# The last two tiles of a mixture-of-experts combine move to TensorE, their loads go in halves from two queues, and the written order of all steps is new

## The reference

```python
x = x + attention(layernorm(x), ...)                 # 16 heads, low-rank q and kv, rotary, causal softmax
x = x + smooth_quant_mlp(layernorm(x), fside, ctx)   # per batch: two int8 products, gate and up, then down
x = x + moe(layernorm(x), ...)                       # 32 experts, top 4 of 3 groups, and a shared MLP
```

```python
s = sqrt(max(amax_x, EPS) / max(amax_w, EPS))        # per column, over rows of x and of w
xs, ws = x / s, w * s
x_scale = max(max(abs(xs), axis=-1), EPS) / 127      # a maximum of each row of x
w_scale = max(max(abs(ws), axis=-1), EPS) / 127      # and of each row of the weights
out = round(xs / x_scale) @ round(ws / w_scale).T * x_scale * w_scale.T
```

## Time and profile before

| | us |
|---|---|
| median of 3 runs (lowest, highest) | 394.71 (391.9, 395.4) |
| the profiled execution, its own time | 394.67 |
| its span, first to last instruction | 392.8 |
| PE busy | 326.6 |
| DVE busy | 263.9 |
| ACT busy | 173.8 |
| POOL busy | 100.5 |

### The profile page before, as it was taken

How to read it: one execution, slowest core, us unless ns; L and a number is a source line. 1 busy time by engine, 2 the same in 40 slices (tenths; PEclk the granted TensorE clock), 3 DMA queues, 4 the chain that set the end, 5 groups by cost and what they waited for, 6 DMA issues and landing times.

```text
span 392.8 us, 6578 instructions
## 1 busy us (share of the span) xinstructions
PE 326.6 (83%) x2000; PEld 230.0 (59%) x2000; DVE 263.9 (67%) x1066; ACT 173.8 (44%) x538; POOL 100.5 (26%) x144
## 2 busy tenths in 40 slices
PE   1898999799999789898899899669684897989880
PEld 0555566566866556766566675447573775655660
DVE  2337686775578778788997778795686478334327
ACT  1233566677446755345786435772042230223100
POOL 4112212231030112025233005330016302545500
PEclk9899999999999989999999999999899798999995
DMA  7999592020000000000000000062000400090175
GB/s 261 332 408 361 166 393 112 0 81 2 2 2 0 2 2 2 0 1 26 14 9 5 2 1 2 15 236 81 0 2 3 138 13 0 7 331 18 32 238 195
DMA packets 17895, 34.28 MB, mean 87 GB/s; under 512 B 4780, under 2 KB 9513, under 8 KB 17220
## 3 DMA queue, kind: packets, MB, share of 16 engines
q1 hardware_dynamic: 15556, 32.66, 24.0%
q0 software_dynamic: 2304, 1.20, 1.1%
HBM read 27.10 MB, written 11.99 MB: 100 GB/s over the span
## 4 chain that ended last, share of the span: by engine, by line
PE 52%; DVE 16%; issue 15%; ACT 6%; POOL 5%; DMA 4%; SPq 1%; another core or an unknown queue 0%; POOLq 0%; DVEq 0%; ACTq 0%
PE psum L527 41%; PE psum L536 11%; DVE x_residual L1526 2%; POOL expert_rows L1612 2%; DMA region_a<-token_parts 2%; DVE region_t L1176 1%; DMA x_residual<-in_x_dram 1%; ACT region_t L933 1%; ACT region_r L881 1%; DVE region_t L1184 1%; DVE region_t L1174 1%; POOL rstd L1571 1%; DVE bn_stats L1074 1%; ACT region_t L931 1%; DVE region_t L1165 1%
## 5 line engine op out<-in xcount | busy, mean ns | idle before, releaser
L527 PE MATMUL psum<-region_h,region_b 128*128 128x256 f32 (+1 forms) x320 | 66.4, 343 | 3.4 <-ACT region_b L881 2.2
L527 PE MATMUL psum<-region_c,region_h 128*128 128x512 f32 x128 | 61.6, 606 | 0.5 <-issue 0.5
L931 ACT ACTIVATE region_t<-region_t,neg_max 128x128 f32<-128x128 f32 x64 | 25.6, 399 | 65.4 <-DVE neg_max L1176 65.0
L527 PEld LDWEIGHTS psum<-region_h,region_b 128*128 128x128 f32 x320 | 47.0, 191 | 11.2 <-issue 4.4
L1583 POOL TENSOR_TENSOR q_chunk<-q_chunk,q_rope_tmp 128x256 f32<-128x256 f32 x32 | 23.5, 734 | 110.3 <-DVE q_chunk L1155 110.2
L1612 POOL DMA_INDIRECT expert_rows<-h_moe,slot_scatter x32 | 32.5, 1016 | 25.4 <-issue 14.4
L536 PE MATMUL psum<-consts,region_t 128*128 128x128 f32 x192 | 32.2, 277 | 6.5 <-DVE region_t L1184 3.1
L527 PEld LDWEIGHTS psum<-region_c,region_h 128*128 128x128 f32 x128 | 23.2, 195 | 18.9 <-issue 18.0
L536 PEld LDWEIGHTS psum<-consts,region_t 128*128 128x128 f32 x192 | 23.0, 141 | 17.6 <-issue 12.4
L933 ACT ACTIVATE region_t<-region_t,neg_max 128x256 f32<-128x256 f32 x64 | 31.6, 494 | 0.0
L527 PE MATMUL psum<-w_folded_out,region_g 128*128 128x256 f32 x128 | 29.8, 381 | 0.0
(11 more groups left out here) (189 smaller groups left out, 616.0 us busy)
## 6 DMA issues: line engine op xcount, KB each, us to landing
region_a<-in_experts_dram SPq DMA_DIRECT2D x17, 384.0 KB, 5.9
region_b<-in_experts_dram SPq DMA_DIRECT2D x10, 384.0 KB, 6.1
region_a<-in_fold_dram SPq DMA_DIRECT2D x3, 1152.0 KB, 12.9
token_parts<-region_g SPq DMA_DIRECT2D x12, 256.0 KB, 6.0
region_a<-token_parts SPq DMA_DIRECT2D x6, 512.0 KB, 6.8
region_c<-in_experts_dram SPq DMA_DIRECT2D x5, 384.0 KB, 3.4
expert_rows<-region_g SPq DMA_DIRECT2D x10, 132.5 KB, 11.1
region_h<-expert_rows SPq DMA_DIRECT2D x5, 256.0 KB, 3.8
```

The source lines that it names most:

```text
L527: return nc.tensor.matmul(out_, lhsT, rhs, start=first, stop=last)
L931: nc.scalar.activation(pr[:, 0:P], pr[:, 0:P], ACT.Exp, bias=nmax[:, hn, 0:1], scale=-1.0, accum_out=sums[:, hn, 0:1])
```

## The change

1. The tiles 4 and 5 (`SUMMED`) are no longer added by `combine.4`. A step `weigh.0` has DVE make 8 diagonal matrices, the identity times the tokens' weights for one k, and `sum.t` is 4 products on PE, diagonal k by the rows of k, summed in PSUM, and one addition on DVE.
2. Each tile's load from `token_parts` is two DMAs, ranks k = 0, 1 and ranks k = 2, 3, with a semaphore each. Even tiles are loaded and stored by SP, odd ones by ACT. Who reads waits for each half.
3. `x_back` has 6 parts in place of 4: maximum, scaling and reciprocal of the rows, then the same for the weights, and `x_qscale` waits for each.
4. `ORDER` is new in the whole. Among it: `slot_weights` stands behind `send.3`, `gate_up.3` and `down.1`; `xpT.2` behind `s_down.2`; `send.3` behind `send.2`; `down.3` ahead of `gate_up.5`; `down.5` ahead of `hidT.6`; 13 one-hots behind `gate_up.7` in place of 12.

The diff in its core (the old and the new text of the order are cut to parts of their ends):

```diff
+SUMMED = (4, 5)
...
-r_pos.3 dispatch r_slots.3 r_slots.3+1 r_slots.3+2 r_slots.3+3 r_slots.3+4 scatter.3.0 send.0 s_add.2 s_add.3
-send.1 gate_up.0 gate_up.1 hidT.0 send.2 scatter.3.1 scatter.3.2 scatter.3.3 scatter.3.4 scatter.3.5 scatter.3.6
-scatter.3.7 gate_up.2 hidT.1 down.0 slot_weights send.3 gate_up.3 hidT.2 down.1 gate_up.4 hidT.3 down.2 send.4
-gate_up.5 hidT.4 down.3 gate_up.6 hidT.5 down.4 onehot.0 onehot.1 onehot.2 onehot.3 gate_up.7 hidT.6 down.5
-onehot.4 onehot.5 onehot.6 onehot.7 hidT.7 down.6 onehot.8 onehot.9 onehot.10 onehot.11 down.7 onehot.12
-onehot.13 onehot.14 onehot.15 combine.0 mix.6 combine.2 mix.7 combine.4
...
+r_weights.2+2 r_weights.2+3 r_weights.2+4 x_back.3 x_back.3+1 s_silu.0 r_weights.2+5 x_back.3+2 x_back.3+3
+s_gate.1 r_pos.2 s_mul.0 s_down.0 x_back.3+4 x_back.3+5 x_qscale.3 scatter.2.0 r_slots.2 r_slots.2+1 x_round.3
...
+r_weights.3+1 r_weights.3+2 r_weights.3+3 r_weights.3+4 r_weights.3+5 r_pos.3 dispatch r_slots.3 r_slots.3+1
+r_slots.3+2 r_slots.3+3 r_slots.3+4 scatter.3.0 scatter.3.1 scatter.3.2 scatter.3.3 send.0 s_add.2 s_add.3
+send.1 gate_up.0 gate_up.1 gate_up.2 hidT.0 scatter.3.4 scatter.3.5 hidT.1 scatter.3.6 scatter.3.7 send.2 send.3
+gate_up.3 down.0 hidT.2 down.1 slot_weights hidT.3 send.4 gate_up.4 down.2 down.3 gate_up.5 hidT.4 gate_up.6
+hidT.5 onehot.0 onehot.1 down.4 onehot.2 gate_up.7 down.5 onehot.3 onehot.4 onehot.5 onehot.6 onehot.7 onehot.8
+hidT.6 down.6 hidT.7 down.7 onehot.9 onehot.10 onehot.11 onehot.12 onehot.13 onehot.14 onehot.15 weigh.0
+combine.0 mix.6 combine.2 mix.7 sum.4 sum.5
...
-         "x_back": 4, "x_gate": 4, "x_smooth2": 3, "x_back2": 3, "x_mm2": 2,
+         "x_back": 6, "x_gate": 4, "x_smooth2": 3, "x_back2": 3, "x_mm2": 2,
...
+        weigh = reg_t[:, 0:len(SUMMED) * TOPK * P].rearrange("p (t k m) -> p t k m", t=len(SUMMED), k=TOPK)
+        ld_parts = [[sem(f"ld_parts{t}_{half}") for t in range(SCATTERED)] for half in range(2)]
...
-            for t in range(SCATTERED):
-                sp.dma_start(parts[:, t, :], pv[t]).then_inc(ld_parts[t], 16)
+            for t in range(0, SCATTERED, 2):
+                for half in range(2):
+                    c0 = half * TOPK * D // 2
+                    sp.dma_start(parts[:, t, c0:c0 + TOPK * D // 2], pv[t][:, c0:c0 + TOPK * D // 2]
+                                 ).then_inc(ld_parts[half][t], 16)
...
+                elif kind == "sum":
+                    t, = a
+                    pe.wait_ge(sg["weigh_ready"], 1)
+                    wait_empty(pe, step)
+                    for k in range(TOPK):
+                        if k % 2 == 0:
+                            pe.wait_ge(ld_parts[k // 2][t], 16)
+                        last = mm(bank(step)[:, 0:D], weigh[:, SUMMED.index(t), k, :], parts[:, t, k * D:(k + 1) * D],
+                                  k == 0, k == TOPK - 1)
+                    fills(last, step)
...
-                    act.wait_ge(sg["inv_ready"], b + 1)
...
+                        act.wait_ge(sg["inv_ready"], 2 * b + 1 + i)
...
+                elif kind == "weigh":
+                    wait_filled(act, ("dn", NG_E - 1))
+                    act.wait_ge(sg["parts_scattered"], 16 * NPAIR)
+                    pv = parts_dram.rearrange("(t p k) d -> t p (k d)", p=P, k=TOPK)
+                    for t in range(1, SCATTERED, 2):
+                        for half in range(2):
+                            c0 = half * TOPK * D // 2
+                            nc.scalar.dma_start(parts[:, t, c0:c0 + TOPK * D // 2], pv[t][:, c0:c0 + TOPK * D // 2]
+                                                ).then_inc(ld_parts[half][t], 16)
+
+            ov = out.rearrange("b (j p) d -> p (b j) d", p=P)
+            for i, t in enumerate(FINISHED):
+                if t % 2 == 1:
+                    act.wait_ge(sg["combined"], i + 1)
+                    nc.scalar.dma_start(ov[:, t, :], xres[:, t, :]).then_inc(sg["out_stored"], 16)
...
-                        last = v.tensor_reduce(sm[:, b, 10 + 2 * i:12 + 2 * i],
-                                               bank(item).rearrange("p (j d) -> p j d", j=2), AX.X, ALU.max,
-                                               apply_absolute_value=True)
-                    yield link(last)
-                    yield link(v.tensor_scalar(sm[:, b, 10:14], sm[:, b, 10:14], EPS_Q, 1.0 / QMAX, ALU.max, ALU.mult))
-                    v.reciprocal(sm[:, b, 14:18], sm[:, b, 10:14]).then_inc(sg["inv_ready"], 1)
+                        o = 10 + 2 * i
+                        yield link(v.tensor_reduce(sm[:, b, o:o + 2], bank(item).rearrange("p (j d) -> p j d", j=2),
+                                                   AX.X, ALU.max, apply_absolute_value=True))
+                        yield link(v.tensor_scalar(sm[:, b, o:o + 2], sm[:, b, o:o + 2], EPS_Q, 1.0 / QMAX,
+                                                   ALU.max, ALU.mult))
+                        v.reciprocal(sm[:, b, o + 4:o + 6], sm[:, b, o:o + 2]).then_inc(sg["inv_ready"], 1)
...
+                elif kind == "weigh":
+                    dve.wait_ge(sg["token_weights_ready"], B)
+                    wait_filled(dve, ("dn", NG_E - 1))
+                    for i, t in enumerate(SUMMED):
+                        for k in range(TOPK):
+                            last = v.tensor_scalar(weigh[:, i, k, :], ident, wtok[:, t, k:k + 1], None, ALU.mult)
+                    last.then_inc(sg["weigh_ready"], 1)
+                elif kind == "sum":
+                    t, = a
+                    wait_filled(dve, step)
+                    v.tensor_tensor(xres[:, t, :], bank(step)[:, 0:D], xres[:, t, :], ALU.add
+                                    ).then_inc(sg["combined"], 1)
...
-                            if k == 0:
-                                dve.wait_ge(ld_parts[t], 16)
+                            if k % 2 == 0:
+                                dve.wait_ge(ld_parts[k // 2][t], 16)
```

147 lines of the change are left out of this document (72 added, 75 removed).

## The result

Over four runs the changed kernel took 400.26 us (median; 398.92 to 400.94), the kernel before 393.30 us beside it; the ratio is 1.0135, 95% interval 1.0089 to 1.0181. It is slower by 7.0 us by the medians; forecast were 5.2 us less. The profiled executions say 399.0 against 392.8 us of span, 6.2 us more.

The account below looks back on a forecast made before the run. PE's nearly full queue was taken to bound the body; scatter, loads and DVE's combine the end. Scatter at 371.2, loads 10.9 and 5.5 us more end at 387.6, 5.2 us sooner: 389.5 us, range 386.0 to 394.5.

Parts of the forecast that it names:

- the cover that send.3 was said to have: Expert stage: PE's 1.33 us wait for send.3 would go, covered by over 3 us of down.0, hidT.2 and down.1.
- the body: Attention work before the tail: new order is a shuffle of neighbours, value 0, bounds -3 to +3 us.
- parts 1 to 6: Kernel's end: DVE's combine relieved, first halves, loads become the end, PE sums 5.5 us behind last landing, load rate, weights hidden.
- the loads: End: twelve half loads of token_parts from two queues, last landing 10.9 us after the scatter, against 11.9 before.
- The clock rival: End: PE idles 2 us or more before the sums, which run at half clock; time 393.1 us, chance 0.22.
- The scatter lands 3.1 us sooner: Router and expert stages: the last scatter into token_parts lands at 371.2; bounds 1 to 3.7 us sooner.
- another core or an unknown queue: Chain of waits: 1.54 us ahead of ACT's copy of group 5, unexplained; its full return was in the 1 us bound.
- xpT.2 moved: Before batch 3's router: moving xpT.2 behind its transposes shortens the sequence by 0.8 us, of which 0.6 kept.
- The smoothing: Rows and weights scaling on DVE: 0.35 us more per batch, yet no effect on time; bounds -0.8 and +0.5 us.
- The slower rival: Body: moved groups' first steps wait for input in PE's queue, some 3 us each with clock falls; 399 us, chance 0.08.

Follow-up runs that it names:

- e2: Order and smoothing of the kernel before, with only the new end (diagonal weights, sums on PE, half loads and stores from two queues): 394.36 us, ratio 1.0024 to before.
- e3: Changed code with the new order up to the step tail and the old order from it on: 395.95 us, ratio 1.0040 to the kernel before.
- e5: Changed code with the old order up to dispatch and the new order from dispatch on (expert stage): 397.25 us, ratio 1.0054 to the kernel before.
- e6: Changed code with the new order up to dispatch and the old order from dispatch on: 396.52 us, ratio 1.0014 to the kernel before.
- e9: Changed code in the old order, but the second half of the expert stage (from hidT.3) in the new order: 396.18 us, ratio 1.0010 to the kernel before.
- e11: Changed code in the old order, but the stretch from tail to dispatch in the new order: 395.09 us, ratio 1.0004 to the kernel before.
- e16: Changed kernel with one body step, norm.55, moved ahead of the second half of x_back.2: 397.65 us, ratio 1.0102 to the kernel before.
- e1: All of the changed code, but in the order of the kernel before: 393.71 us, ratio 0.9989 to the kernel before.
- e8: Changed kernel without the eight indirect DMAs of scatter.3, so that batch's slot records are missing: 395.49 us, ratio 1.0019 to the kernel before.
- e13: Changed code in the old order, with slot_weights moved behind down.1: 391.76 us, ratio 0.9953 to the kernel before.

## Why the prediction was wrong

Of the sum, two steps failed: the cover that send.3 was said to have, and the body, put at nothing. The forecast's terms and what the two profiles show:

| | forecast | measured |
|---|---|---|
| body, to r_T.2 | 0 | +5.2 |
| r_T.2 to the first send | -0.6 | -1.3 |
| first send to the last scatter | -2.5 | +3.5 |
| from there to the end | -2.1 | -1.2 |
| span | -5.2 | +6.2 |

*The end* (parts 1 to 6). The end came 5.5 us behind the landing that released PE, as worked out; the weights are hidden, 1.68 us for at most 2.7; DVE has no part in it. The first halves were in 4.1 us after the scatter's landing, not 3, which cost nothing, since DVE was not last. The term that was mis-sized is the loads: SP's took 11.8 us and all twelve 12.1, not 10.9, so 1.2 us were gained from the last scatter on instead of 2.1. By the Trainium skill (DMA: Bandwidth & Descriptors, Issuing engines are not separate DMA queues) a second issuing engine saves only the time of issuing. The trace agrees, in that the loads took no less than the 11.9 us of before; no run has two queues without halves, so what each does alone isn't shown.

*The clock rival.* In the after profile PE idled 2.23 us ahead of the sums and they ran at full clock. In e2, e3, e5, e6, e9 to e11 and e16, with 2.65 to 4.39 us of idle time, they ran partly at half (e11 5.77 us for 4.1): the rival's mechanism is real and takes 1 to 2 us when it comes. The idle time alone does not decide it: e1 idled 2.95 us and kept the full clock.

*The scatter lands 3.1 us sooner.* This step failed. 0.6 us of the 3.1 is xpT.2's and 2.5 us the experts'; counted from the first send the scatter came 3.5 us later. The sentence that failed is "Its cover is down.0, hidT.2 and down.1, over 3 us; gone." In the new order these three stand behind gate_up.3, not ahead of it, so they cover nothing: the wait for region_g grew from 1.33 to 2.59 us. The other half is what it waits for. The row "another core or an unknown queue", left as unexplained and bounded on the gain's side only, was a late signal of PE. Before, send.3 ran behind scatter.3's row and its signal was 0.01 us late (342.94); with the sends together it runs beside that row, and the signals of send.2 and send.3 are 3.08 and 1.45 us late (343.04, 344.76). Without scatter.3's DMAs this wait is gone, but the stage is only 1.3 us shorter (e8). slot_weights was priced too low too (POOL started 22.1 us after the first send, against 20.8), but e13 shows that alone this costs nothing.

*xpT.2 moved, 0.6 us.* The profile has 1.4 us less to r_T.3, and e11 about as much; in e11 it is given back when the clock falls behind it.

*The smoothing.* Right: nothing (e1 against e2, and their stages against before).

*The body, 0 within 3 us.* This step failed too: 5.2 us in the profile, 0.9 to 2.3 in the others with the new body and no idle matmuls, and 2.2 us by the medians of e3 and e1. So the 5.2 us is in part the bad luck of one execution. The bound counted waits, one more or less with a half clock behind it. PE's idle time did not grow; three stretches at half clock made PE's own work longer. Which wait brings them stays open. The slower rival had the place (body) and half the mechanism, without the experts, at 0.08.

## What to carry to other kernels

An in-order queue asks, for each step behind which another engine's answer is awaited, what stands directly behind it: follow the new order literally and write the cover's position down, because one step (down.0) in another place went with 5 us of a stage between two profiles, about half of it half clock, and with 0.5% of the kernel between two ratios whose intervals overlap. A row that says "unknown queue" or "remote" is a wait that can grow; find its neighbours (here POOL's indirect DMAs) before moving work into it. Where a program runs with short idle gaps on TensorE, compare orders stage by stage over several profiles, as half-clock stretches move single executions by more than the edits do.

## What was unexpected in the hardware

PE's completion signals arrive up to 5.6 us late while POOL issues a row of indirect DMAs 1.28 us apart, and most of the late ones come in a burst when the row has landed (342.01 to 342.30 before, with the last landing at 341.93); without the DMAs the lag is gone (e8). It takes more than such a row: beside the seven of scatter.2 (298.83 to 307.68 before), of the five matmul signals from there to 309.7 three were seen within 0.01 us, and two have no matching event; in e8 all five were seen within 0.01 us. What else is needed wasn't found.
